# Item tables moved behind the ranks with four segments, and products in pairs on two halves of TensorE's rows

## The chip, the cores and the metric

The kernel runs on one core of one Trainium2 chip. The metric is the device time of one execution in microseconds; the lower the better. TensorE is PE in the profile, with PEld for its weight loads, VectorE is DVE, ScalarE is ACT, GpSimd is POOL and SyncE is SP.

## The reference

A small graph network with 6250 nodes of 256 features and 100000 edges, sorted by destination. Cut to what matters here:

```python
x = x + L0_gnn(layernorm(x), src, dst, edge_weight)      # weighted sum of neighbours, two products, L2 norm
x = x + L0_ffn(layernorm(x))                             # shared MLP and 4 gated experts
# L1 gnn, on the normalised x; edge_index[0] is src, all nodes have batch 0
sums = segment_sum(edge_attr, src, num_segments=n)       # 64 attributes per edge, summed by source
counts = segment_sum(ones, src, num_segments=n)
edge_attr_agg = sums / maximum(counts, 1.0)[:, None]
combined = concatenate([x, edge_attr_agg, u[batch]], axis=1)
x = x + (relu(combined @ W1 + b1) @ W2 + b2)             # 448 -> 512 -> 256
x = x + L1_ffn(layernorm(x))                             # 8 experts, the best 2 of each row
```

## The kernel before

**Rows and edges.** Nodes stand in 49 tiles of 128 (`NT`), in seven groups of seven (`NG`, `G`). Edges stand in 784 columns of 128 (`NC`), a run is four columns (`RUN`). An item is one run against one tile: the run's edges are made one-hot over the tile's 128 nodes by VectorE, PE multiplies the one-hot with the edges' rows, and VectorE adds the product to the tile's sum. A run with edges of several tiles is several items.

**The first block: aggregation by destination.** GpSimd gathers the source rows of a run from DRAM (L341, an indirect DMA per column) into one of seven slots (`SLOTS`), ScalarE weighs them (L401), VectorE makes the one-hots (`onehots`, L546) and sums (L558), PE multiplies (`products`, L649). GpSimd gathers into a slot again when PE has done with the run before in it (`s_mm` against row 3 of `row_i`). A loop step is eight items (`RING`). Steps run to item 96 (`FIRST`), then to 200 (`UNTIL`), then to 248 (`NI_A`).

Beside this work the edges are ranked by source. ScalarE counts the edges below each tile's first node (`source_count`, L391), in each segment of the columns (`SEGMENTS`) apart. After item 96 VectorE turns the counts into starts and offsets, and for each of three segments it makes the item tables: `runs_of_tiles`, `item_tables` (about 20 small instructions), PE turns two columns of `tab` into a row (`in_rows`, L628), VectorE copies it to `row4_i`. PE's steps from item 96 on wait for `s_row` 2, which follows the third table. Then, from item 96 to 200, VectorE makes four ranks in each step (`ranks`: a mask L595, one scan in each segment L598, a copy L603), 52 in all. SyncE loads the first attributes after `s_rank` 1 and stores the tables after `s_row` 2. GpSimd starts the first 16 scatters behind its gathers.

**The second block: dense layers beside the scatter.** GpSimd scatters the edges' attributes, one column of 128 edges per indirect DMA (L894, 768 times), into `sorted_edges` in DRAM, by rank; meanwhile the other engines do the layers L0. Then comes the aggregation by source: ScalarE's queue loads sorted edges (L1015, 16 slots `STEP4`), VectorE makes one-hots (L1347) and sums (L1356), PE multiplies (L1179). Each segment is sorted by itself, so its loads may start once its columns have landed (`LANDED`), and it has as many items as runs plus `NT` - 1 = 48: 160, 104 and 76, in sum `NL` = 340. ScalarE waits for a segment's columns before the steps of 16 items from `ITS4_FROM[n]` on:

```python
ITS4_FROM = tuple(sum(ITEMS4[:n]) // STEP4 for n in range(len(SEGMENTS)))
```

**The third block: the second GNN and the experts.** For each group g of seven tiles: ScalarE spreads the reciprocals of the counts (L1607), PE's `reciprocals` (L1705) brings them into the shape of the sums, VectorE's `node_columns` (L1840) multiplies them into the means, 64 partitions (`EA`) by 512 and 384 nodes. PE's `hidden` (L1715) multiplies the means, four times 128 outputs by two halves of the nodes, into four banks of PSUM, VectorE adds the parts made earlier (`add_parts`, L1846), ScalarE applies the ReLU (L1613), and PE's `node` (L1729) makes a tile's output, 28 products in a group. VectorE adds it to x (L1857), takes statistics (L1849, L1865) and makes the experts' gates; ScalarE writes the rows normalised by these (`gate_rows`, L1620), in its queue ahead of the next group's ReLUs. SyncE loads an expert's second weights in each group (`second_weights`, L1453), the parts (L1457), and stores x. Then follow the experts' blocks up to the end.

Of the kernel before, what the change touches and what calls it, by code (L numbers as in the profile page):

```python
# [6 lines left out]
P = 128  # L7
# [4 lines left out]
G = 7  # L12
# [29 lines left out]
SEGMENTS = ((0, 448), (448, 672), (672, NC))  # L42
# [77 lines left out]
def build(nc, a, out):  # L120
# [9 lines left out]
    with ctx:  # L130
# [77 lines left out]
        if True:  # L208
# [26 lines left out]
            starts = sb("starts", [P, NB + 1], f32, ph)  # L235
# [42 lines left out]
            with nc.Block() as block:  # L278
                @block.sync
                def _(sp):  # L280
# [17 lines left out]
                    sp.wait_ge(s_row, 2)  # L298
# [119 lines left out]
                def _(dve):  # L418
# [53 lines left out]
                    def runs_of_tiles(edges_per_run):  # L472
                        shift = edges_per_run.bit_length() - 1
                        own.add(nc.vector.tensor_copy(st_i[:, :], starts[:, :]))
                        own.add(nc.vector.tensor_scalar(up_i[:, :], starts[:, :], float(edges_per_run - 1), None, ALU.add))
                        own.add(nc.vector.tensor_tensor(nz[:, :], starts[:, 1:NB + 1], starts[:, 0:NB], ALU.is_gt))
# [99 lines left out]
                    for n, (c0, c1) in enumerate(SEGMENTS):  # L576
                        own.add(nc.vector.tensor_copy(starts[:, :], psum[:, 0, n * P:n * P + NB + 1]))
                        own.sync()
                        own.add(nc.vector.tensor_tensor(base[:, n, 0:NB], psum[:, 1, n * P:n * P + NB], starts[:, 0:NB], ALU.add))
                        own.sync()  # L580
                        own.add(nc.vector.tensor_scalar(base[:, n, 0:NB], base[:, n, 0:NB], float(c0 * P - 1), None, ALU.add))
                        runs_of_tiles(P * RUN)
                        item_tables(c0 // RUN, c1 // RUN)
                        dve.sem_inc(s_tab, 1)
                        dve.wait_ge(s_tabT, 2 + n)
                        i0, i1 = sum(ITEMS4[:n]), sum(ITEMS4[:n + 1])
                        own.add(nc.vector.tensor_copy(row4_i[:, :, i0:i1], psum[0:1, 2 + n, :].rearrange("p (k i) -> p k i", k=2)[:, :, 0:i1 - i0]))
                        own.sync()
# [23 lines left out]
                    with dve.Fori(UNTIL // RING, NI_A // RING) as it:  # L612
# [3 lines left out]
                def _(pe):  # L616
# [41 lines left out]
                    last.then_inc(s_off, 1)  # L658
                    for n in range(len(SEGMENTS)):
                        pe.wait_ge(s_tab, 2 + n)  # L660
                        in_rows(2 + n, (0, 1)).then_inc(s_tabT, 1)
                    pe.wait_ge(s_row, 2)
# [1456 lines left out]
```

## Time and profile before

| | us |
|---|---|
| median of 3 runs | 3086.56 |
| lowest, highest | 3085.42, 3093.0 |
| the profiled execution | 3096.71 |
| its span | 3095.0 |
| PE busy | 2492.1 |
| POOL busy | 1833.0 |
| DVE busy | 1404.5 |
| ACT busy | 927.9 |

The span goes from the first to the last instruction of the profiled execution; its time holds a little more. A busy share is a mean over stages with different limits: what an instruction is worth is read in its own stage, from the wait that ends last there. A line of the timeline gives the start, the duration, the engine, the line in the kernel, the operation and how many it merges, and in brackets how long the engine stood idle before it and what ended that.

### The profile page before, as it was taken

The page shows a single profiled execution, that of the slowest core. Times are in us where ns is not written, and L with a number is a line of the kernel's source. Part 1 is how long each engine was busy: PE and PEld are TensorE (multiplying, and loading weights), DVE is VectorE, ACT ScalarE, POOL GpSimd, SP SyncE. Part 2 cuts the span into 40 slices and gives each one's busy share as a digit, 9 for nine tenths or more (in the row PEclk, how much of TensorE's full clock was granted, in tenths as well). Part 3 has the DMA queues.
Part 4 walks back from the last instruction along what each step waited for, and adds up shares of the span by engine and source line. Part 5 has one row for each costly group of instructions (what it writes and reads, how often), then busy time and mean ns, then how long its engine had stood idle before and what let it go on. Part 6 is the DMA issues. An engine that isn't in the chain of part 4 may idle for free. (4 is left out here: it accounts for less than half of the span.)

```text
span 3095.0 us, 48451 instructions
## 1 busy us (share of the span) xinstructions
PE 2492.1 (81%) x11766; PEld 1963.1 (63%) x11767; DVE 1404.5 (45%) x3627; ACT 927.9 (30%) x2240; POOL 1833.0 (59%) x1907
## 2 busy tenths in 40 slices
PE   2556665666667589999999795839989999999998
PEld 1344444544555456666665794837668888888898
DVE  5222224988863233433433794836783222222222
ACT  4665333333333234444343000001542111111122
POOL 6777777777777777777777777770355222222222
PEclk9778776788888789999999897968999999999999
DMA  6333334333333312222222674632675444444464
GB/s 244 105 104 104 104 104 125 105 104 104 104 105 104 99 55 75 69 75 79 75 79 75 187 196 124 200 94 83 225 251 148 120 105 117 122 106 117 117 175 136
DMA packets 216588, 372.91 MB, mean 120 GB/s; under 512 B 50437, under 2 KB 133694, under 8 KB 215231
## 3 DMA queue, kind: packets, MB, share of 16 engines
q0 software_dynamic: 82928, 157.51, 19.2%
q1 hardware_dynamic: 75772, 154.16, 15.2%
q10 hardware_dynamic: 57812, 60.35, 6.7%
q8 instruction: 33, 0.54, 0.1%
q14 instruction: 43, 0.35, 0.0%
HBM read 290.16 MB, written 81.71 MB: 120 GB/s over the span
## 5 line engine op out<-in xcount | busy, mean ns | idle before, releaser
L649 PE MATMUL psum<-arena 128*128 x1984 | 621.6, 478 | 361.1 <-ACT arena L401 341.6
L341 POOL DMA_INDIRECT arena<-xn_rows,arena x784 | 747.4, 953 | 249.4 <-issue 234.8
L894 POOL DMA_INDIRECT sorted_edges<-arena x768 | 742.2, 966 | 249.0 <-issue 226.6
L649 PEld LDWEIGHTS psum<-arena 128*128 128x128 f32 x1984 | 463.7, 241 | 518.9 <-issue 436.1
L401 ACT ACTIVATE arena<-arena 128x256 f32<-128x256 f32 x784 | 334.0, 496 | 578.0 <-DMA arena<-xn_rows,arena 578.0
L1179 PE MATMUL psum<-arena,acc 128*65 128x128 f32 x2720 | 312.7, 277 | 107.9 <-DVE arena L1347 107.7
L1179 PEld LDWEIGHTS psum<-arena,acc 128*65 128x65 f32 x2720 | 301.6, 140 | 118.8 <-DVE arena L1347 112.0
L1347 DVE SCALAR_TENSOR_TENSOR arena<-psum,acc 128x512 f32<-128x512 f32 x340 | 252.8, 744 | 110.8 <-DMA acc<-sorted_edges 93.2
L1778 PE MATMUL psum<-arena,xr 128*128 x1344 | 299.1, 381 | 2.0 <-DVE xr L2008 2.0
L1765 PE MATMUL psum<-xr 128*128 128x256 f32 x1344 | 299.6, 381 | 0.9 <-DVE xr L2002 0.9
L558 DVE TENSOR_TENSOR acc<-acc,psum 128x256 f32 x248 | 103.1, 416 | 431.6 <-PE psum L649 431.6
L1765 PEld LDWEIGHTS psum<-xr 128*128 128x128 f32 x1344 | 257.1, 191 | 36.7 <-DVE xr L2002 1.3
L1778 PEld LDWEIGHTS psum<-arena,xr 128*128 128x128 f32 x1344 | 253.1, 191 | 35.5 <-issue 2.4
L1547 POOL DMA_INDIRECT out_y_dram<-xr,acc x84 | 130.9, 1558 | 217.7 <-ACT xr L1656 204.2
L546 DVE SCALAR_TENSOR_TENSOR arena<-psum,arena 128x512 f32<-128x512 f32 x252 | 187.7, 746 | 46.1 <-issue 37.5
L2008 DVE TENSOR_SCALAR xr<-psum,arena 128x256 f32<-128x256 f32 x168 | 73.6, 479 | 231.2 <-PE psum L1765 229.8
L1094 PE MATMUL psum<-arena 128*128 128x512 f32 (+1 forms) x336 | 158.3, 636 | 0.0
L1532 POOL DMA_INDIRECT dispatched<-acc,arena x98 | 94.4, 963 | 107.8 <-DVE arena L1902 62.2
L1656 ACT ACTIVATE xr<-xr,acc 128x256 f32<-128x256 f32 x84 | 42.6, 508 | 348.6 <-DVE xr L2014 348.6
L1607 ACT ACTIVATE arena<-ident,rcount 128x128 f32<-128x128 f32 x49 | 15.0, 387 | 437.1 <-PEq L818 427.0
L1542 POOL COPY acc<-acc 128x18 f32<-128x18 f32 x43 | 8.6, 200 | 217.6 <-DVE xr L2002 211.4
L2014 DVE TENSOR_TENSOR xr<-psum,acc 128x256 f32<-128x256 f32 x84 | 35.6, 424 | 218.9 <-PE psum L1778 218.9
(318 smaller groups left out, 3147.7 us busy)
## 6 DMA issues: line engine op xcount, KB each, us to landing
xr<-in_f_W_dram SPq DMA_DIRECT2D x63, 1024.0 KB, 5.1
acc<-sorted_edges ACTq DMA_DIRECT2D x340, 132.0 KB
arena<-in_attr_dram SPq DMA_DIRECT2D x98, 264.0 KB, 2.8
arena<-xn_rows,arena POOLq DMA_INDIRECT x784, 2.7
sorted_edges<-arena POOLq DMA_INDIRECT x784
arena<-hidden_parts SPq DMA_DIRECT2D x7, 1792.0 KB, 8.5
arena<-dispatched SPq DMA_DIRECT2D x42, 265.0 KB, 2.7
arena<-in_f_W_dram SPq DMA_DIRECT2D x8, 1024.0 KB, 11.5
```

The lines of the kernel that those rows point to most:

```text
L341: pool.indirect_dma_start(out=rows[:, c, :], out_offset=None, in_=xn_d, in_offset=bass.IndirectOffsetOnAxis(ap=idx[:, c:c + 1], axis=0)).t ...
L401: last = nc.scalar.activation(row, row, ACT.Copy, scale=w_c[:, ds((it * SLOTS + u) * RUN + c, 1)])
L546: nc.vector.scalar_tensor_tensor(hot[:, u, :, :], iota_p.unsqueeze(1).to_broadcast([P, RUN, P]), tile_b0[:, ds(i, 1)], dst_c[:, ds((run - ...
L558: nc.vector.tensor_tensor(there, there, psum[:, bank(u), 0:D], ALU.add).then_inc(s_acc, 1)
L649: last = nc.tensor.matmul(psum[:, bank(u), 0:D], hot[:, u, c, :], rows[:, ds(slots[k] + c, 1), :].squeeze(1), start=c == 0, stop=c == RUN - 1)
L894: pool.indirect_dma_start(out=edges_d, out_offset=bass.IndirectOffsetOnAxis(ap=pos_i[:, c:c + 1], axis=0), in_=stage[:, q % PARTS, c % SC, ...
L1094: last = nc.tensor.matmul(psum[:, b + m % 3, 0:w], w1[:, j, m, :], yT[:, j, columns(c)], start=j == 0, stop=j == 1)
L1179: last = nc.tensor.matmul(psum[0:EA + 1, bank4(u), 0:P], rows4[:, u, c, 0:EA + 1], hot4[:, u % RING, c, :], start=c == 0, stop=c == RUN - 1)
L1347: nc.vector.scalar_tensor_tensor(hot4[:, u % RING, :, :], iota4.unsqueeze(1).to_broadcast([P, RUN, P]), tile_b[:, ds(it * STEP4 + u, 1)], ...
L1547: pool.indirect_dma_start(out=out["y"], out_offset=bass.IndirectOffsetOnAxis(ap=wide_meta[:, u, h, 0:1].bitcast(i32), axis=0), in_=wide_y[ ...
L1765: last = nc.tensor.matmul(psum[:, 1 + m // 2, m % 2 * W:(m % 2 + 1) * W], wide_w[:, u, c, m * P:(m + 1) * P], wide_xT[:, c, :], start=c == ...
L1778: last = nc.tensor.matmul(psum[:, 5 + h, 0:D], wide_hT[:, m, h * P:(h + 1) * P], fw2[:, ds(e, 1), m, :].squeeze(1), start=m == 0, stop=m = ...
```

## The change

The columns are cut into four segments, 512, 128, 64 and 80 columns, with 176, 80, 64 and 68 items, in sum 388. The starts, offsets and bases of all segments are made after item 96 as before; the item tables are made after item 200, one after each of four steps of eight items, turned in a bank of PSUM that the ranks no longer need. `starts` is kept for each segment. SyncE waits for `s_row` 3 before it stores the tables; attributes are loaded as before after `s_rank` 1.

In the third block SyncE first copies the sums of groups 1 to 6 from partitions 0 to 63 to partitions 64 to 127 (`twice`), six DMAs. `reciprocals` brings the reciprocals to 128 partitions, `node_columns` scales both copies and waits in group 1 for the six DMAs. The weights `gw1e` are loaded twice, one copy for each half. In groups 1 to 6 every second product of `hidden` takes the upper half of rows. Products 5 and 7 no longer wait for a sum; products 4 and 6 wait for two.

```diff
-SEGMENTS = ((0, 448), (448, 672), (672, NC))
+SEGMENTS = ((0, 512), (512, 640), (640, 704), (704, NC))
...
-                    sp.wait_ge(s_row, 2)
+                    sp.wait_ge(s_row, 3)
                     sp.dma_start(item_d.unsqueeze(0), row4_i[:, :, :]).then_inc(s_rst, 16)
...
                     for n, (c0, c1) in enumerate(SEGMENTS):
-                        own.add(nc.vector.tensor_copy(starts[:, :], psum[:, 0, n * P:n * P + NB + 1]))
-                        own.sync()
-                        own.add(nc.vector.tensor_tensor(base[:, n, 0:NB], psum[:, 1, n * P:n * P + NB], starts[:, 0:NB], ALU.add))
-                        own.sync()
+                        own.add(nc.vector.tensor_copy(starts[:, n, :], psum[:, 0, n * P:n * P + NB + 1]))
+                    own.sync()
+                    for n, (c0, c1) in enumerate(SEGMENTS):
+                        own.add(nc.vector.tensor_tensor(base[:, n, 0:NB], psum[:, 1, n * P:n * P + NB], starts[:, n, 0:NB], ALU.add))
+                    own.sync()
+                    for n, (c0, c1) in enumerate(SEGMENTS):
                         own.add(nc.vector.tensor_scalar(base[:, n, 0:NB], base[:, n, 0:NB], float(c0 * P - 1), None, ALU.add))
-                        runs_of_tiles(P * RUN)
-                        item_tables(c0 // RUN, c1 // RUN)
-                        dve.sem_inc(s_tab, 1)
-                        dve.wait_ge(s_tabT, 2 + n)
-                        i0, i1 = sum(ITEMS4[:n]), sum(ITEMS4[:n + 1])
-                        own.add(nc.vector.tensor_copy(row4_i[:, :, i0:i1], psum[0:1, 2 + n, :].rearrange("p (k i) -> p k i", k=2)[:, :, 0:i1 - i0]))
-                        own.sync()
+                    own.sync()
                     dve.sem_inc(s_row, 1)
                     dve.sem_inc(s_rank, 1)
...
-                    with dve.Fori(UNTIL // RING, NI_A // RING) as it:
+                    for n, (c0, c1) in enumerate(SEGMENTS):
+                        for half in range(2):
+                            products(UNTIL + n * RING, half)
+                        runs_of_tiles(P * RUN, n)
+                        item_tables(c0 // RUN, c1 // RUN)
+                        dve.sem_inc(s_tab, 1)
+                        dve.wait_ge(s_tabT, 2 + n)
+                        i0, i1 = sum(ITEMS4[:n]), sum(ITEMS4[:n + 1])
+                        own.add(nc.vector.tensor_copy(row4_i[:, :, i0:i1], psum[0:1, RING - 2, :].rearrange("p (k i) -> p k i", k=2)[:, :, 0:i1 - i0]))
+                        own.sync()
+                    dve.sem_inc(s_row, 1)
+                    with dve.Fori(UNTIL // RING + len(SEGMENTS), NI_A // RING) as it:
...
+                    pe.wait_ge(s_row, 2)
+                    with pe.Fori(FIRST // RING, UNTIL // RING) as it:
+                        products(it)
                     for n in range(len(SEGMENTS)):
+                        products(UNTIL // RING + n)
                         pe.wait_ge(s_tab, 2 + n)
-                        in_rows(2 + n, (0, 1)).then_inc(s_tabT, 1)
-                    pe.wait_ge(s_row, 2)
-                    with pe.Fori(FIRST // RING, NI_A // RING) as it:
+                        in_rows(RING - 2, (0, 1)).then_inc(s_tabT, 1)
+                    with pe.Fori(UNTIL // RING + len(SEGMENTS), NI_A // RING) as it:
                         products(it)
...
+            twice = sums[0:2 * EA, :, :]
...
+                    for g in range(1, NG):
+                        sp.dma_start(twice[EA:2 * EA, g * G:(g + 1) * G, :], twice[0:EA, g * G:(g + 1) * G, :]).then_inc(s_deg_in, 16)
...
-                            nc.tensor.matmul(psum[0:EA, n, 0:c1 - c0], ones[:, 0:EA], spread[:, c0 // P:c1 // P, :].rearrange("p k n -> p (k n)"),
+                            nc.tensor.matmul(psum[0:2 * EA, n, 0:c1 - c0], ones[:, 0:2 * EA], spread[:, c0 // P:c1 // P, :].rearrange("p k n -> p (k n)"),
...
-                            if q >= 4:
-                                pe.wait_ge(s_hadd, g * 8 + q - 3)
-                            mean = aggT[0:EA, ds(g * G + c0 // P, (c1 - c0) // P), :].rearrange("p k n -> p (k n)")
-                            nc.tensor.matmul(psum[:, 4 + q % 4, 0:c1 - c0], gw1e[:, m, :], mean, start=True, stop=True).then_inc(s_h5, 1)
+                            if q >= 4 and q % 2 == 0:
+                                pe.wait_ge(s_hadd, g * 8 + q - 2)
+                            low = EA * (q % 2) if g else 0
+                            mean = twice[low:low + EA, ds(g * G + c0 // P, (c1 - c0) // P), :].rearrange("p k n -> p (k n)")
+                            nc.tensor.matmul(psum[:, 4 + q % 4, 0:c1 - c0], gw1e[low:low + EA, m, :], mean, start=True, stop=True).then_inc(s_h5, 1)
...
+                            if g == 1:
+                                dve.wait_ge(s_deg_in, 32 + 16 * (NG - 1))
+                            high = 2 * EA if g else EA
```

## Rows read from the trace of the kernel before

**Rows 1.** The waits of all engines: us in total, times, longest us.
```profile
DVE arena L1347 <- DMA acc<-sorted_edges: 93.2, 2, 55.2
...
POOL arena L341 <- PE psum L649: 14.6, 37, 3.6
```

**Rows 2.** The timeline around the item tables: start us, us, engine, line.
```profile
487.76 3.78 PE L649 MATMUL psum<-arena 128*128 x8 [3.04 <-ACT arena L401]
...
500.74 1.87 PE L628 MATMUL psum<-ident,arena 128*1 128x128 f32 x8 [4.59 <-DVEq L584]
...
518.18 12.15 PE L649 MATMUL psum<-arena 128*128 x41 [2.13 <-ACT arena L401]
...
522.74 0.95 POOL L341 DMA_INDIRECT arena<-xn_rows,arena  x1 [3.64 <-PE psum L649]
```

**Rows 3.** The timeline of the aggregation by source, VectorE.
```profile
1727.66 3.79 DVE L1347 SCALAR_TENSOR_TENSOR arena<-psum,acc 128x512 f32<-128x512 f32 x5
...
1913.92 0.75 DVE L1347 SCALAR_TENSOR_TENSOR arena<-psum,acc 128x512 f32<-128x512 f32 x1 [38.01 <-DMA acc<-sorted_edges]
...
2058.67 0.75 DVE L1347 SCALAR_TENSOR_TENSOR arena<-psum,acc 128x512 f32<-128x512 f32 x1 [55.20 <-DMA acc<-sorted_edges]
...
2138.08 0.28 DVE L1356 TENSOR_TENSOR acc<-acc,psum 65x128 f32 x1 [0.21 <-DVE acc L1356]
```

**Rows 4.** Groups by line, VectorE, from 2077.7 to 2122.1 and 2003.5 to 2139.
```profile
L1347 DVE SCALAR_TENSOR_TENSOR arena<-psum,acc 128x512 f32<-128x512 f32 x48 | 35.7, 743 | 2.4 <-PE psum L1179 1.9
...
L1347 DVE SCALAR_TENSOR_TENSOR arena<-psum,acc 128x512 f32<-128x512 f32 x84 | 62.5, 743 | 59.3 <-DMA acc<-sorted_edges 55.2 <-PE psum L1179 2.5 <-issue 0.6
```

**Rows 5.** The timeline of the third node group.
```profile
2204.92 6.25 PE L1715 MATMUL psum<-acc 64*128 64x512 f32 x16 [0.68 <-DVE xr L1857]
...
2206.73 5.03 DVE L1846 TENSOR_TENSOR arena<-psum,arena 128x512 f32<-128x512 f32 x8
...
2206.85 3.55 ACT L1620 ACTIVATE acc<-xr,arena 128x256 f32<-128x256 f32 x7 [0.47 <-DVE arena L1870]
...
2210.31 4.57 ACT L1613 ACTIVATE arena<-arena 128x512 f32<-128x512 f32 x8
...
2211.10 1.72 PE L1705 MATMUL psum<-arena,ones 128*64 128x512 f32 x4
...
2212.91 7.00 PEld L1729 LDWEIGHTS psum<-arena 128*128 128x128 f32 x32 [0.75 <-ACT arena L1613]
...
2226.81 6.25 PE L1715 MATMUL psum<-acc 64*128 64x512 f32 x16 [0.68 <-DVE xr L1857]
```

**Rows 6.** The rank stretch: busy us of PE, PEld, DVE, ACT, POOL; PEclk; DMA.
```profile
530.00:700.00 170.00, 113.04 (x377) 86.96 (x375) 145.96 (x214) 58.90 (x145) 128.60 (x135) 0.80 0.36 104
```

**Rows 7.** Groups by line, GpSimd, from 1063 to 1950 and 1915 to 2000.
```profile
L894 POOL DMA_INDIRECT sorted_edges<-arena x687 | 663.9, 966 | 223.3 <-issue 204.0 <-DMA sorted_edges<-arena 18.9 <-POOL arena L881 0.4
...
L894 POOL DMA_INDIRECT sorted_edges<-arena x66 | 63.8, 966 | 23.3 <-issue 21.7 <-DMA sorted_edges<-arena 1.6
```

**Rows 8.** Timeline of the first node group; DMA issues (KB, us to landing).
```profile
2143.30 0.40 SPq L1453 DMA_DIRECT2D arena<-in_f_W_dram  x1
...
2168.40 0.68 DVE L1840 TENSOR_TENSOR acc<-acc,psum 64x512 f32<-64x512 f32 x1 [1.34 <-PE psum L1705]
...
arena<-hidden_parts SPq DMA_DIRECT2D x7, 1792.0 KB, 8.5
```

**Rows 9.** Timeline of PE in groups five and six; two stretches of six.
```profile
2264.29 5.61 PE L1729 MATMUL psum<-arena 128*128 128x264 f32 x24
...
2288.05 7.28 PE L1729 MATMUL psum<-arena 128*128 128x264 f32 x24
...
2284.60:2288.00 3.40, 1.94 (x11) 1.34 (x9) 2.85 (x18) 1.49 (x2) 2.49 (x4) 1.00 1.01 354
...
2288.00:2291.40 3.40, 3.39 (x11) 2.73 (x11) 3.37 (x18) 0.00 (x0) 0.53 (x1) 0.65 0.74 269
```

**Rows 10.** The timeline of the first node group, PE.
```profile
2150.27 3.25 PE L1705 MATMUL psum<-arena,ones 128*64 128x512 f32 x4 [0.82 <-DVE arena L1833]
```

More of the change, by code:

```diff
@@ L234, in build @@
             cnt = sb("cnt", [P, len(SEGMENTS), NB], f32, ph)
-            starts = sb("starts", [P, NB + 1], f32, ph)
+            starts = sb("starts", [P, len(SEGMENTS), NB + 1], f32, ph)
             st_i = sb("st_i", [P, NB + 1], i32, ph)
@@ L471, in _, with runs_of_tiles @@
                     own.sync()
-                    def runs_of_tiles(edges_per_run):
+                    def runs_of_tiles(edges_per_run, n):
                         shift = edges_per_run.bit_length() - 1
-                        own.add(nc.vector.tensor_copy(st_i[:, :], starts[:, :]))
-                        own.add(nc.vector.tensor_scalar(up_i[:, :], starts[:, :], float(edges_per_run - 1), None, ALU.add))
-                        own.add(nc.vector.tensor_tensor(nz[:, :], starts[:, 1:NB + 1], starts[:, 0:NB], ALU.is_gt))
+                        own.add(nc.vector.tensor_copy(st_i[:, :], starts[:, n, :]))
+                        own.add(nc.vector.tensor_scalar(up_i[:, :], starts[:, n, :], float(edges_per_run - 1), None, ALU.add))
+                        own.add(nc.vector.tensor_tensor(nz[:, :], starts[:, n, 1:NB + 1], starts[:, n, 0:NB], ALU.is_gt))
                         own.sync()
@@ L744, in build @@
             run6 = sb("run6", [P, NX], f32, ph6)
[L745 removed]
+            gw1e = spare[0:2 * EA, 3 * G * ED + D:3 * G * ED + D + 4 * P].rearrange("p (m n) -> p m n", m=4)
             u0 = sb("u0", [P, 1], f32, ph6)
@@ L854, in _ @@
                         for dst, src in (
-                            (gw1e[:, :, :], a["g_W1"][D:D + EA, :].rearrange("p (m n) -> p m n", n=P)),
+                            (gw1e[0:EA, :, :], a["g_W1"][D:D + EA, :].rearrange("p (m n) -> p m n", n=P)),
+                            (gw1e[EA:2 * EA, :, :], a["g_W1"][D:D + EA, :].rearrange("p (m n) -> p m n", n=P)),
                             (gw1u, a["g_W1"][D + EA:D + EA + P, :].rearrange("p (m n) -> p m n", n=P)),
@@ L900, in _ @@
                         pool.wait_ge(s_hxo[c], NG * 16)
-                    pool.wait_ge(s_w3, 16 * (19 + 10))
+                    pool.wait_ge(s_w3, 16 * (19 + 11))
                     for g in range(NG):
@@ L1599, in _ @@
                 def _(act):
-                    act.wait_ge(s_w3, 16 * (19 + 10))
+                    act.wait_ge(s_w3, 16 * (19 + 11))
                     def deviation(ln, g, s_v, s_sd):
@@ L1691, in _ @@
                 def _(pe):
-                    pe.wait_ge(s_w3, 16 * (19 + 10))
+                    pe.wait_ge(s_w3, 16 * (19 + 11))
                     for m in range(4):
@@ L1838, in node_columns @@
                             dve.wait_ge(s_t5, PHASES * 2 + g * 2 + n + 1)
-                            mean = aggT[0:EA, ds(g * G + c0 // P, (c1 - c0) // P), :]
-                            nc.vector.tensor_tensor(mean, mean, psum[0:EA, n, 0:c1 - c0].rearrange("p (k n) -> p k n", n=P), ALU.mult).then_inc(s_tc5, 1)
+                            if g == 1:
+                                dve.wait_ge(s_deg_in, 32 + 16 * (NG - 1))
+                            high = 2 * EA if g else EA
+                            mean = twice[0:high, ds(g * G + c0 // P, (c1 - c0) // P), :]
+                            nc.vector.tensor_tensor(mean, mean, psum[0:high, n, 0:c1 - c0].rearrange("p (k n) -> p k n", n=P), ALU.mult).then_inc(s_tc5, 1)
                     def add_parts(g):
```

1 line of the change is left out of this document (removed).

## The prediction, on record before the result

> **What bounds the kernel now.** I read the page first, for the order of the stages: GpSimd is 70% or more busy in two long stretches, the gathers of node rows and the scatters of edge attributes, and PE is near full in the rest. Then came the waits, to see where each of the two parts of the change touches a queue that somebody waits for.
>
> First, the item tables. In the gather stage the GpSimd queue sets the pace: its longest wait for PE is 3.6 us, and the other waits charged to PE are the usual 0.30 us between two gathers [rows 1]. The reader is to see that the one long wait has a place: PE's products stop at 491.54 (487.76 + 3.78) and go on at 518.18, and GpSimd, which may run seven slots ahead, stops until 522.74 [rows 2]. In between VectorE makes three sets of tables and PE turns each into rows; one turn takes PE 1.87 us [rows 2].
>
> Second, the aggregation by source. VectorE idles 93.2 us in two waits for sorted edges, the second 55.2 us long [rows 1]; it starts again at 2058.67 and ends at 2138.36 [rows 3]. All that comes after the last scatter lies bare on the path, while the items before it are hidden behind the scatters. The group of lines after 2003.5 shows 84 one-hot instructions [rows 4]. The last segment has 28 + 48 = 76 items; the rest comes from `ITS4_FROM`, which divides 264 by 16 and rounds down to 16, so that the loads of items 256 to 263 stand behind the last wait too. 48 items from 2077.7 to 2122.1 took 44.4 us, so 0.926 us for one [rows 4].
>
> Third, the node groups of the second GNN. One group lasts 21.89 us (2204.92 to 2226.81) [rows 5]. PE's eight products L1715 take 6.25 us and its reciprocals L1705 end at 2212.82, but the next work, L1729 at 2212.91, is released by ScalarE's fourth ReLU: ScalarE writes seven rows (L1620, 3.55 us, from 2206.85) and only then the ReLUs (L1613, from 2210.31) [rows 5]. VectorE's eight sums L1846 run without a gap, 5.03 us from 2206.73 [rows 5]. So two engines other than PE set this stretch, and PE is level with ScalarE to within 0.09 us.
>
> **The change, part by part.**
>
> Tables moved. The stop of PE shrinks from 26.6 us to the offsets alone. From the last product before it to the first turn are 9.2 us (491.54 to 500.74), with the first table in them [rows 2]; two small products and a few copies come on top, which I put at 1 us, so the stop is at most some 10 us. One of 26.6 us cost GpSimd 3.34 us beyond its usual 0.30 [rows 2]: seven slots swallow some 23 us, and one of 10 us costs nothing: **-3.3 us**. Bounds: 0 (if another stall takes its place) and -3.6. The tables now stand behind the ranks, each after eight items. PE waited 4.59 us for one and took 1.87 us to turn it [rows 2], so a stop is 6.5 us, and far below the 23 us of the slots. The four are eight items apart, over which PE catches up. Without that cover they would cost 4 x 6.5 = 26 us. Behind the waiting VectorE stand the sums that free PE's banks, behind PE the slots. SyncE now holds the store of the tables until the fourth; only the attribute loads stand before it, and the store comes with 16 items still to go, before the stage's end.
>
> Four segments in ranks and counts. Each rank has one scan more, over the same columns in sum, so only its fixed part is added. No row shows that alone; below it is 0, above it is the mean of all of VectorE's instructions there, 146.0/214 = 0.68 us [rows 6]. An iteration of four ranks and eight items has 36 instructions, so 170 us hold 5.9 of them, each 28.6 us with 24.6 busy. Even at the upper end, 4 x 0.68 = 2.7 us fit into the 4.0 that are free: hidden behind the gathers, 0 us. Without that cover the upper end would cost 13 x 2.7 = 35 us, and GpSimd would feel only what the seven slots don't swallow. One Sign and accumulation more per count on ScalarE is hidden too, as that engine waits for gathered rows between its runs.
>
> Four segments in the aggregation. Items rise from 340 to 388, with 176, 80, 64 and 68; all the borders are multiples of 16, so the rounding is gone. Behind the last wait stand 68 instead of 84: 16 x 0.926 = **-14.8 us**. The 64 more before it (320 for 256) need cover. VectorE starts at 1727.66 [rows 3], now 3.3 us earlier, at 1724.4, and 320 x 0.926 = 296 us later, at 2020.7, it would be done, 35 us before the last edges (2058.67 - 3.3 = 2055.4). Are the middle segments there in time? By 1950 GpSimd had begun 687 scatters after the first 16, one in 1.291 us [rows 7]. Columns 512, 640 and 704 are then issued at 1704, 1869 and 1951, less 3.3; the loads of items 176, 256 and 320 wait for the columns 640, 704 and 784, and the items come up at 1887, 1961 and 2021. Each has 13 us or more, but the last. If a middle segment were late the 35 us would take it.
>
> Loads and scatters share the DMA engines. With loads beside them, 66 scatters have 63.8 + 23.3 = 87.1 us, 1.32 us each, against 1.291 over the whole [rows 7]. The loads now run 64 x 0.926 = 59 us longer beside them, some 46 scatters: between 0 and 46 x 0.03 = 1.4 us. The stretch of 85 us itself gives 1.29, so I stay near the low end, **+0.5 us**.
>
> The copies. SyncE issues six copies of aggregated means, 64 partitions by 3584 bytes, 224 KB each, 1.3 MB in sum, ahead of the expert's weights, from 2143.30 [rows 8]. VectorE's second call of `node_columns` waits for all. Before, it came at 2168.40 [rows 8], 25.1 us later. 1792 KB of hidden parts take 8.5 us [rows 8]; with six issues of some 0.5 us and the weights behind them I put landing at 10 to 15 us, hidden, 0 us. Bounds: no gain, and a loss only above 25 us; without the cover the 10 to 15 us would be bare. `node_columns` on 128 partitions instead of 64 costs as many columns, so the same.
>
> The pairs. If two products on the two halves of rows run beside each other, PE saves up to half of 6.25 us in each of six groups, 19 us of work. But by rows 5 the next products wait for ScalarE at 2212.91, whatever PE does before; the saving gives 0 (0.09 x 6 = 0.5 at most). If they do not run side by side, nothing changes either: the coarser waits of products 4 and 6 ask for sums that end at 2208.0 and 2209.3, and the last product is still done before its sum at 2211.1. The Trainium skill, TensorEngine Tiling (Array Packing), Performance Considerations, says that such tiling speeds up TensorE but not the evacuation of PSUM, which can then be the bottleneck. By this rule the part is worth nothing as well; the trace agrees, with 5.03 us of sums without a gap.
>
> What the pairs can cost is the clock. A pair takes 6.25/8 = 0.8 us. PE would work two pairs, stand until 2208.0, work the other two with a gap between, then 1.7 us of reciprocals, then stand some 1.3 us for ScalarE: 4 x 0.8 + 1.7 = 4.9 of 8.0 us in which it is now all but full. In the sixth group PE stood still for 1.46 us, was busy 1.94 of 3.40 us, and the granted clock then read 0.65: 24 records of L1729 took 7.28 us instead of 5.61, **1.67 us** [rows 9]. A fall in each of the six groups would cost 10 us, none 0. The gaps are spread, not one, so I take the near end, one fall more: **+1.7 us**. The skill's page TensorE: Matmul & The Clock Gate, section HAM oscillation, names such a pattern of short bursts and waits as what makes the clock swing; by it the six falls would be the forecast, -7.6 instead of -15.9.
>
> Sum: -3.3 - 14.8 + 0.5 + 1.7 = **-15.9 us**. The profiled execution took 3096.71 us, of which 3095.0 are span: it would take 3080.8. It lies 10.2 above the median of the runs shown, 3086.56, so the median is expected at **3070.7 us**.
>
> **The rivals.**
>
> A: the clock falls in most groups. For it: [rows 9], and the drop in PE's busy share. Against: a fall is only seen where PE was idle 43% of a stretch, and half of what it slows is cover. Time: 3086.56 - 17.6 + 10.0 = 3079.0.
>
> B: the pairs do shorten the groups, since PE and ScalarE are level and VectorE's chain starts sooner. For it: PE ends only 0.09 us before ScalarE lets it go. Against: L1620 and four ReLUs do not depend on L1715. 6 x 3.1 = 18.7 us: 3070.7 - 18.7 - 1.7 = 3050.3.
>
> C, to the other side: the clock falls and stays low for whole groups. In the first group it is low from 2150 on although PE is all but full, and L1705 takes 3.25 us there against 1.72 [rows 5, 10]. A group's 56 records of L1729, at 5.61 us for 24, are 13.1 us [rows 9] and would take as much again; six of them 79: 3086.56 - 17.6 + 79 = 3148. It makes the kernel slower by over 0.3% from 17.6 + 9.3 = 27 us on, which is a little over two whole groups. Against it: the one fall of [rows 9] cost 1.67 us and not a group.
>
> D: the segment part does nothing, as a middle segment comes late or the last is loaded slowly. Then only the 3.3 us stay, less 1.7 and 0.5: 3085.5. Against: 35 us of cover.
>
> **How the numbers follow.** 0.3% (9.3 us) is about what a measurement of this kernel can tell from no change. Chances: forecast 0.66 (its own range 3066 to 3075), A 0.18, B 0.07, C 0.03, D 0.06. Forecast and B lie beyond 0.3%, and of A the part with falls in three to five groups, 0.12: faster 0.85; the rest of A and D: same 0.12; C: slower 0.03. The range goes from 3063 (no fall, and a little of B) to 3079 (A with all six falls); it leaves out most of B, C, D, and the ends of A.
>
> **What would show it.** After the change: no wait of `L341` for PE above 0.5 us; 68 one-hots after the last wait for edges, which is 30 to 38 us long; the end of the aggregation 16 to 20 us earlier; L1715 starting its last product sooner but L1729 still released by the ReLUs, and a group of 21.9 us, up to 1.7 more where the clock falls. I am wrong if a wait for `s_deg_in` shows at `node_columns`, if a middle segment shows a wait over 1 us, or if groups change by more than 2 us.

## The result, and the profile after

The kernel after takes 3071.73 us (median of 12 runs, 3063.92 to 3077.27), the kernel before 3090.64 us on the same chips (12 runs, 3081.32 to 3096.02). The ratio is 0.9937, with a 95% interval of 0.9926 to 0.9947: 19.5 us less (16.4 to 22.9). Forecast were 3070.7 us and a gain of 15.9, a ratio of 0.9948. The time lies in the range, 1.0 us above the forecast, and the gain is 3.0 us (by the medians, 18.9) to 3.6 us (by the ratio) larger than the sum said. The ratios and their intervals are an estimate over all the runs and can differ from the quotient of two medians, by up to 0.0015 in what follows. The profiled execution took 3076.77 us, with a span of 3074.7; the span before was 3095.0, so the two profiles are 20.3 us apart.

The waits of all engines after, as in [rows 1] (us in total, times, longest us):

```profile
DVE arena L1359 <- DMA acc<-sorted_edges: 32.1, 1, 32.1
...
POOL arena L341 <- PE psum L656: 11.0, 36, 0.3
```

One wait for edges is left out of two, and GpSimd's long wait for PE is gone. The timeline at the offsets, which answers to [rows 2]:

```profile
487.81 1.99 PE L656 MATMUL psum<-arena 128*128 x8 [1.69 <-ACT arena L401]
...
495.60 3.18 SPq L297 DMA_DIRECT2D arena<-in_attr_dram  x7
...
497.22 7.16 PE L656 MATMUL psum<-arena 128*128 x24 [3.63 <-issue]
...
504.62 3.39 ACT L401 ACTIVATE arena<-arena 128x256 f32<-128x256 f32 x8 [6.72 <-DMA arena<-xn_rows,arena]
505.94 0.95 POOL L341 DMA_INDIRECT arena<-xn_rows,arena  x1 [1.77 <-issue]
```

PE's products stop for 7.4 us (487.81 + 1.99 to 497.22) where they stopped for 26.6. But GpSimd has a new gap of 1.77 us at 505.94. Just before it ScalarE waits 6.72 us for gathered rows, and before that SyncE issues the seven loads of edge attributes. The tables behind the ranks, PE:

```profile
920.00 1.36 PE L635 MATMUL psum<-ident,arena 128*1 128x128 f32 x8 [4.30 <-DVEq L613]
...
948.51 1.86 PE L635 MATMUL psum<-ident,arena 128*1 128x128 f32 x8 [4.32 <-DVEq L613]
```

The four turns wait 4.19 to 4.32 us each, 27 to 29 us apart. The aggregation by source, which answers to [rows 3], and the group of its one-hot instructions from 2024 to 2120, which answers to [rows 4]:

```profile
1727.79 2.73 DVE L1359 SCALAR_TENSOR_TENSOR arena<-psum,acc 128x512 f32<-128x512 f32 x4
...
2054.57 0.75 DVE L1359 SCALAR_TENSOR_TENSOR arena<-psum,acc 128x512 f32<-128x512 f32 x1 [32.08 <-DMA acc<-sorted_edges]
...
2119.10 0.28 DVE L1368 TENSOR_TENSOR acc<-acc,psum 65x128 f32 x1 [0.21 <-DVE acc L1368]
```

```profile
L1359 DVE SCALAR_TENSOR_TENSOR arena<-psum,acc 128x512 f32<-128x512 f32 x68 | 50.6, 744 | 35.3 <-DMA acc<-sorted_edges 32.1 <-issue 2.0 <-PE psum L1191 0.9
```

From the last wait to the end are 64.8 us (2054.57 to 2119.38) instead of 79.7. The timeline of the third node group after, which answers to [rows 5]:

```profile
2186.99 1.99 PE L1730 MATMUL psum<-acc 64*128 64x512 f32 x8 [0.68 <-DVE xr L1875]
...
2188.79 4.51 DVE L1864 TENSOR_TENSOR arena<-psum,arena 128x512 f32<-128x512 f32 x8
...
2190.13 0.92 PE L1730 MATMUL psum<-acc 64*128 64x384 f32 x4 [1.16 <-DVE arena L1864]
...
2192.18 1.77 PE L1719 MATMUL psum<-arena,ones 128*128 128x512 f32 x4
2192.37 4.57 ACT L1627 ACTIVATE arena<-arena 128x512 f32<-128x512 f32 x8
...
2194.97 7.41 PE L1744 MATMUL psum<-arena 128*128 128x264 f32 x32 [1.02 <-ACT arena L1627]
...
2208.87 1.13 PE L1730 MATMUL psum<-acc 64*128 64x512 f32 x4 [0.68 <-DVE xr L1875]
```

The pairs do run side by side: the first four products take 1.99 us, where four of the same 512 columns took some 3.6 (their share by columns of the 6.25 for eight). PE then stands twice for VectorE, 1.16 and 0.28 us, and 1.02 us for ScalarE's ReLU. The group lasts 21.88 us (2186.99 to 2208.87), as before. The copies, which answer to [rows 8]:

```profile
2124.39 4.89 SPq L1465 DMA_DIRECT2D acc<-acc  x6
...
2149.71 0.69 DVE L1858 TENSOR_TENSOR acc<-acc,psum 128x512 f32<-128x512 f32 x1 [1.45 <-PE psum L1719]
```

Nobody waits for them: the reader 25.3 us later is released by PE.

The 20.3 us between the profiles come together so. The last gather comes 1.5 us earlier (1033.0 for 1034.5). The scatters take 2.6 us less, so at the last wait it is 4.1. The last segment brings 14.9, so at the end of the aggregation it is 19.0. The first node group is 0.9 us longer (29.75 for 28.87), four groups are equal, the sixth is 2.3 shorter (23.16 for 25.44), and 0.1 to 0.2 go either way behind and before them.

### The profile page after: what moved, and what is told of

The parts are those of the page before. It is cut to its first block and busy times, and to the rows that moved or that the text cites. A ratio compares the mean times of both kernels' runs of the same rounds, so it can differ in the third digit from the quotient of the medians.

```text
span 3074.7 us, 50036 instructions
## 1 busy us (share of the span) xinstructions
PE 2517.9 (82%) x12162; PEld 1993.4 (65%) x12163; DVE 1454.9 (47%) x3798; ACT 941.9 (31%) x2340; POOL 1833.4 (60%) x1907
## 3 DMA queue, kind: packets, MB, share of 16 engines
q1 hardware_dynamic: 76332, 155.66, 15.4%
## 5 line engine op out<-in xcount | busy, mean ns | idle before, releaser
L1191 PE MATMUL psum<-arena,acc 128*65 128x128 f32 x3104 | 354.7, 276 | 46.6 <-DVE arena L1359 46.4
L1191 PEld LDWEIGHTS psum<-arena,acc 128*65 128x65 f32 x3104 | 340.6, 139 | 60.6 <-DVE arena L1359 50.8
L1359 DVE SCALAR_TENSOR_TENSOR arena<-psum,acc 128x512 f32<-128x512 f32 x388 | 288.4, 744 | 50.0 <-DMA acc<-sorted_edges 32.1
```

The source lines that it names most:

```text
L1191: last = nc.tensor.matmul(psum[0:EA + 1, bank4(u), 0:P], rows4[:, u, c, 0:EA + 1], hot4[:, u % RING, c, :], start=c == 0, stop=c == RUN - 1)
L1359: nc.vector.scalar_tensor_tensor(hot4[:, u % RING, :, :], iota4.unsqueeze(1).to_broadcast([P, RUN, P]), tile_b[:, ds(it * STEP4 + u, 1)], ...
```

## The experiments

**One part at a time.** Four kernels, each against the kernel before, whose median there was 3091.49. Without the pairs:

```diff
-                            low = EA * (q % 2) if g else 0
-                            mean = twice[low:low + EA, ...]
+                            mean = aggT[0:EA, ...]
...
-                    for g in range(1, NG):
-                        sp.dma_start(twice[EA:2 * EA, ...], twice[0:EA, ...])
```

> The change without its second part: four segments and moved tables, but one copy of the means and one product after another. Theory (the pairs lie behind ScalarE's ReLUs and give nothing by themselves): 0.994 to 0.996 of the kernel before, within 3 us of the full change, the end of the aggregation at 2119 as in the full change, and node groups of 21.9 us; the sixth group may fall into the low clock again and be 25.4 us instead of 23.2. Rival (the pairs give what the result has beyond the forecast): 3 us or more slower than the full change, and longer in every group, not only the sixth.

Measured: 3076.48 us, ratio 0.9954 (0.9939 to 0.9968); one wait of 33.2 us. Its fourth group lasted 26.77 us and not 21.9. The timeline of PE there, and two stretches of it (busy us of PE, PEld, VectorE, ScalarE and GpSimd, granted clock, DMA share, GB/s):

```profile
2202.39 9.76 PE L1725 MATMUL psum<-acc 64*128 64x512 f32 x16 [0.68 <-DVE xr L1867]
2212.08 3.24 PE L1715 MATMUL psum<-arena,ones 128*64 128x512 f32 x4
```

```profile
2203.00:2206.40 3.40, 3.40 (x8) 1.50 (x7) 2.68 (x12) 2.38 (x6) 2.79 (x3) 0.79 0.99 329
2206.40:2209.80 3.40, 3.40 (x6) 1.67 (x5) 1.42 (x3) 3.40 (x8) 2.48 (x4) 0.50 0.48 166
```

The same eight products that take 6.25 us in [rows 5] take 9.76 here, because the granted clock falls to 0.50, the 1.2 GHz level, while PE is busy without a gap. That costs 4.9 us of this profile. By the ratios this kernel is 5 us slower than the whole, outside the 3 us of the theory, but only one group is longer and not every one, as the rival has it.

The segments without tables moved and without pairs, as three segments with the last border at 704:

```diff
-SEGMENTS = ((0, 448), (448, 672), (672, NC))
+SEGMENTS = ((0, 512), (512, 704), (704, NC))
```

> The kernel before with only the borders of its three segments moved, from columns 448 and 672 to 512 and 704; tables where they were, no pairs. 340 items as before, 176, 96 and 68 of them. Theory (only the number of items behind the last wait counts, 84 before and 68 now, each 0.926 us): 14 to 15 us faster, 0.995 to 0.9955; the middle segment is done at some 2042, before the last edges. Rival (a fourth segment is needed to keep the middle items in time): the last wait for edges disappears and the end comes at 2130 or later, less than 9 us faster.

Measured: 3080.53 us, ratio 0.9966 (0.9953 to 0.9979). Its two waits for edges sum to 77.0 us, the longest 63.2, and the last one-hot starts at 2120.4 instead of 2135.4, 15.0 us earlier, so a fourth segment is not needed for this. The ratio gives less than the trace, 10.5 us (6.5 to 14.5), and less than the theory's 0.995 to 0.9955. The profile has a long group, 4.8 us; whether the other runs have one too is not shown:

```profile
2233.50 9.64 PE L1715 MATMUL psum<-acc 64*128 64x512 f32 x16 [0.68 <-DVE xr L1857]
```

The tables behind the ranks, three segments in their old places, no pairs:

```diff
-SEGMENTS = ((0, 512), (512, 640), (640, 704), (704, NC))
+SEGMENTS = ((0, 448), (448, 672), (672, NC))
```

> Only the item tables moved behind the ranks, with the three segments of before, 84 items behind the last wait, no pairs. Theory: the long stop of the gathers goes but for a short one that the attribute loads bring along, 1 to 3 us faster, within 0.1%; the aggregation ends some 1 to 4 us earlier. Rival (moving the tables frees more, up to the scatters): 4 us or more faster.

Measured: 3089.29 us, ratio 0.9992 (0.9981 to 1.0003). The last gather comes at 1032.3, 2.2 us earlier than before, and the last one-hot starts 1.0 us earlier (2134.4). By its time alone the gain can't be told from none.

The pairs alone, on the kernel before (its diff is that of the first experiment, turned round):

> The kernel before with only the second part: copies of the means and products in pairs. Theory: nothing in groups two to five (21.9 us each), and at most 2 to 3 us in the sixth group, where PE waits for VectorE and the clock fell before: between 3 us faster and 1 us slower. Rival A (short bursts of PE let the clock fall): 5 to 10 us slower. Rival B (the groups shorten): 6 us or more faster.

Measured: 3087.5 us, ratio 0.9991 (0.9982 to 0.9999), so 2.8 us less (0.3 to 5.6). The second to the fifth group last 21.88 to 21.89 us, and the sixth 23.37 instead of 25.44, as the theory has it.

The middle values of the parts, 0.9966, 0.9992 and 0.9991, multiply to 0.9949, and the whole is 0.9937 (0.9926 to 0.9947). The intervals of the parts are wide enough for the 0.0012 between them. The segment edit carries most of it.

**All rows of TensorE, one product after another.** (From here to the later border, before: 3095.09.) In all node groups but the first each product of the aggregated means now contracts all 128 partitions, both copies at half value; the sum is the same.

```diff
-                            low = EA * (q % 2) if g else 0
-                            mean = twice[low:low + EA, ...]
+                            high = 2 * EA if g else EA
+                            mean = twice[0:high, ...]
```

> The full change, but in groups 1 to 6 each product of hidden takes all 128 rows (both copies of the means at half their value, both copies of the weights), one after another: PE's work is 6.25 us again, on full rows instead of half. Theory (products on 64 rows let the granted clock fall or keep it low even when PE is busy without a gap, and that is what the pairs save): no group of 26.7 us, all of 21.9 but the sixth, and a time within 2 us of the full change. Rival (the pairs help by freeing PE, or the falls come from elsewhere): the time is that of the change without pairs, 4 to 5 us slower, and groups of 26.7 us are seen.

Measured: 3072.31 us, ratio 0.9941 (0.9923 to 0.9959). A group of it:

```profile
2198.99 6.25 PE L1731 MATMUL psum<-acc 128*128 128x512 f32 x16 [0.68 <-DVE xr L1876]
2205.08 1.67 PE L1720 MATMUL psum<-arena,ones 128*128 128x512 f32 x4
2206.98 7.41 PE L1745 MATMUL psum<-arena 128*128 128x264 f32 x32 [0.23 <-ACT arena L1628]
```

Products on 128 rows take the same 6.25 us as on 64, and with 6.25 us of PE in place of the 3.8 of the pairs (1.99 + 0.92 + 0.92) the group lasts the same 21.88 us. So what PE saves by running side by side does not shorten these groups. Whether full rows keep the clock up this kernel can't tell: single products on 64 rows have no long group in four profiles of six either.

**ReLUs ahead of the row part.** If ScalarE's order is the bound, the pairs pay only once that is changed:

```diff
                     for g in range(1, NG):
                         deviation(ln6, g - 1, s_v6, s_sd6)
+                        hidden(g)
                         gate_rows(g - 1)
-                        hidden(g)
```

> The full change with ScalarE's ReLUs of a group ahead of its writing of the normalised rows of the group before. Theory (ScalarE's rows hide what the pairs save on PE): L1744 starts 7.0 instead of 8.0 us after the first product, groups of some 20.9 us, 4 to 6 us faster than the full change. Rival (another engine bounds the group): groups of 21.9 us, no gain.

> The change without pairs, with the ReLUs first. Theory: PE's eight products and the reciprocals end 7.9 us after the first product, so groups stay at 21.8 us and at most 1 us is gained over the change without pairs; the pairs are worth 5 us or more beside this. Rival: as fast as with pairs.

Measured: with pairs 3068.61 us, ratio 0.9917 (0.9899 to 0.9936); without 3071.45 us, 0.9936 (0.9919 to 0.9952). A group with pairs:

```profile
2184.66 1.99 PE L1730 MATMUL psum<-acc 64*128 64x512 f32 x8 [0.76 <-DVE xr L1875]
...
2187.19 4.58 ACT L1627 ACTIVATE arena<-arena 128x512 f32<-128x512 f32 x8 [1.07 <-DVE arena L1864]
...
2189.85 1.77 PE L1719 MATMUL psum<-arena,ones 128*128 128x512 f32 x4
...
2191.46 7.31 PE L1744 MATMUL psum<-arena 128*128 128x264 f32 x32
...
2205.36 1.99 PE L1730 MATMUL psum<-acc 64*128 64x512 f32 x8 [0.78 <-DVE xr L1875]
```

The wait of L1744 for ScalarE is gone, and a group lasts 20.70 us (2184.66 to 2205.36); without pairs the same order gives 21.73. So ScalarE's order hid 1.2 us of what the pairs save in a group. By the ratios the pairs are worth 6 us here, but the two intervals overlap. Not all of the gain is kept: the four earlier groups save 4.6 us against the kernel after, and the sixth lasts 24.88 us instead of 23.16. In it PE waits longer for VectorE, and the products behind the wait take 7.28 us instead of 5.60:

```profile
2263.21 0.39 PE L1734 MATMUL psum<-arena,ones 128*128 128x8 f32 x2 [2.18 <-DVE arena L1904]
...
2263.84 7.28 PE L1744 MATMUL psum<-arena 128*128 128x264 f32 x24
```

**A later border.** Borders at 512, 640 and 736, with a wait at half a step so that the rounding does no harm (its lines are left out here):

```diff
-SEGMENTS = ((0, 512), (512, 640), (640, 704), (704, NC))
+SEGMENTS = ((0, 512), (512, 640), (640, 736), (736, NC))
```

> The full change with borders 512, 640 and 736, and the loads' wait for a segment's columns at a half step of eight items, so that exactly 60 items stand behind the last columns. Theory: the third segment starts at some 1991, when column 736 has landed, and its 72 items end at some 2058, just after the last columns; the wait there is 0 to 4 us; 60 x 0.926 = 56 us later the aggregation ends, at some 2114, 4 to 6 us before that of the full change. Rival (middle items come late): it ends at 2118 or later, no gain.

Measured: 3074.03 us, ratio 0.9936 (0.9919 to 0.9953). VectorE's only wait has moved to the segment before the last:

```profile
1997.42 0.75 DVE L1365 SCALAR_TENSOR_TENSOR arena<-psum,acc 128x512 f32<-128x512 f32 x1 [35.00 <-DMA acc<-sorted_edges]
```

```profile
L1365 DVE SCALAR_TENSOR_TENSOR arena<-psum,acc 128x512 f32<-128x512 f32 x132 | 98.2, 744 | 40.8 <-DMA acc<-sorted_edges 35.0 <-PE psum L1197 3.7 <-issue 0.7
```

From 1997.42 on, 132 items run without another wait for edges, and the last one-hot starts at 2117.9, where it is 2116.5 in the kernel after: the third segment has become the late one, and the rival holds. Of the two last borders tried, 704 and 736, neither is shown to be faster; borders between them were not tried.

**The last four** (before: 3092.25). The attribute loads of SyncE moved behind the ranks:

```diff
-                    sp.wait_ge(s_rank, 1)
+                    sp.wait_ge(s_rank, 3 * NRANK + 1)
                     for h in range(PARTS):
                         sp.dma_start(stage[:, h, :, :], ...)
```

> The whole change, and SyncE's first seven loads of edge attributes (L297) wait until all ranks are made (s_rank at 3 x NRANK + 1, at 899.9 in the kernel after) instead of for the first 1 (495.60). In the kernel after one gap of GpSimd is left behind the offsets, 1.77 us at 505.94, and ScalarE's runs wait 6.72 us for gathered rows at 504.62, after the attribute loads of 495.60. Theory A, the loads delay the gathered rows: the gap at 506 goes, the last gather comes at 1031.5 (after: 1033.0) and nothing shows near 900, where GpSimd's slots are full again; the whole is 1.5 us shorter, too little to tell by its time. Rival B, the gap is left by PE's stop of 7.4 us at 489.8: it stays at 506, at 1.8 us. Rival C, the gap goes with the loads, wherever they are: 1.5 to 2 us near 900.

Measured: 3068.62 us, ratio 0.9925 (0.9912 to 0.9939), the last gather at 1033.4. The timeline near 900:

```profile
898.70 3.22 SPq L297 DMA_DIRECT2D arena<-in_attr_dram  x7
...
907.57 1.70 ACT L401 ACTIVATE arena<-arena 128x256 f32<-128x256 f32 x4 [7.14 <-DMA arena<-xn_rows,arena]
908.88 0.95 POOL L341 DMA_INDIRECT arena<-xn_rows,arena  x1 [1.92 <-issue]
```

At 506 GpSimd now issues every 1.26 us without a gap, and the gap stands at 908.88, as long as it was. The kernel after has no gap near 909. Rival C is right: the seven loads can take this time from the gathers in both places.

The whole change with three segments:

```diff
-SEGMENTS = ((0, 512), (512, 640), (640, 704), (704, NC))
+SEGMENTS = ((0, 512), (512, 704), (704, NC))
```

> The whole change with three segments of columns, borders 512 and 704, instead of four with 512, 640 and 704: the last segment is the same, 68 items behind the last wait. Theory, the fourth segment gives only cover: VectorE waits twice, 70 to 80 us in sum, the last wait 55 to 65 us instead of 32.1, one-hot products end at 2118 to 2121, and the time is that of the kernel after, ratio to before 0.993 to 0.995. Rival, the segment between is needed, so that the loads of the second segment with 704 columns come too late: one-hots end over 3 us later, ratio 0.9955 or more.

Measured: 3068.73 us, ratio 0.9923 (0.9909 to 0.9937); the waits are 76.8 us in two, the longest 63.6, and the last one-hot starts at 2115.0. No gain of the fourth segment is seen: what counts here is where the last border lies.

The kernel without pairs once more:

> The same kernel as tables_4seg_no_pairs once more: tables behind the ranks and four segments, products of the aggregated means one after another on 64 rows. It asks how often the clock falls within these products. Theory, products on 64 rows are where the clock falls with PE fully busy: a group of 26 to 27 us is seen again in one of groups 1 to 4 (two of the four such profiles so far that don't have the ReLUs first), and the time is 3 to 5 us above the kernel after, ratio to before 0.995 to 0.996. Rival, the two long groups were luck that pairs have as often: all groups 21.9, ratio 0.9935 to 0.9945.

Measured: 3070.29 us, ratio 0.9933 (0.9919 to 0.9946), the second to the fifth group at 21.88 to 21.89 us (the expectations count the groups from 0). The rival holds for this profile.

The ReLUs first, three segments and the late attribute loads together:

> The version that the runs so far point to: pairs, the next group's products of the aggregated means before its row part on every engine's queue as in relu_first_pairs (groups 20.7), three segments with borders 512 and 704, and the attribute loads behind the ranks. If the parts add: ratio to before 0.9915 less 0.0005 for the attribute loads, so 0.991, 3066 to 3069 against a before of 3093; groups of 20.7 us, one-hots end at 2117 to 2119. Rival, the parts don't add (the attribute loads disturb the gathers elsewhere or the second segment is late): 0.993 or more.

Measured: 3071.16 us, ratio 0.9932 (0.9918 to 0.9945). The second to the fifth group last 20.66 to 20.80 us, as meant, but the sixth lasts 26.50 us, and the whole gains nothing. The ratio is the rival's, its causes are not: the last one-hot starts at 2117.6, as the theory has it, and the loss is in the node groups. In that group:

```profile
2261.93 0.55 PE L1734 MATMUL psum<-arena,ones 128*128 128x8 f32 x2 [2.28 <-DVE arena L1904]
...
2262.76 8.59 PE L1744 MATMUL psum<-arena 128*128 128x264 f32 x24
```

```profile
2259.30:2262.70 3.40, 1.12 (x6) 0.77 (x5) 2.88 (x17) 1.49 (x2) 2.64 (x3) 0.90 1.05 363
2262.80:2270.00 7.20, 7.20 (x20) 5.69 (x21) 5.13 (x28) 0.00 (x0) 3.14 (x4) 0.58 0.36 132
```

PE waits 2.28 us for the counts that VectorE makes at the end of its chain for the experts. It is busy 1.12 us of 3.40, the clock falls behind that, and 24 records of L1744 take 8.59 us instead of 5.61. The kernel after has the same wait with 0.74 us and no fall (clock 1.00, records 5.60 us). Of 4.7 us that the earlier groups save, 3.3 go here. The other kernel with pairs and the ReLUs first has the same loss, with 2.18 us of wait and 7.28 us of records. PE is ready for the counts 1.3 us sooner there (14.1 us after the group's start instead of 15.4), but the counts come no sooner, 16.3 to 16.4 us after it. No kernel here is shown to beat the one after. The fastest by its middle value, with the ReLUs first, has an interval up to 0.9936, and this kernel, which contains its edit, did not repeat it.

## Why the prediction was right, point by point

**Tables, -3.3 forecast.** The step that the stop shrinks below what seven slots swallow holds: the stop is 7.4 us, against "at most some 10", the wait for PE of 3.6 us is gone, and the turns behind the ranks (4.2 to 4.3 us of wait, 1.87 of work) show in no wait of GpSimd. The size was off. The last gather gains 1.5 us, not 3.3, since the attribute loads now have a gap of their own, 1.77 us. 1.5 + 1.77 is the 3.3 of the forecast, though a match to the tenth is luck. Of the nine profiles with the tables moved and the loads near 500, three have no such gap, and their last gather comes at 1031.5 to 1031.8, 2.7 to 3.0 us earlier than before; six have one of 0.9 to 2.0 us, and theirs comes at 1032.3 to 1034.2. Without the tables moved it comes at 1034.2 to 1034.8 (three profiles). So the stop itself is worth nearly the 3.3 us, and a collision that comes in most profiles but not in all takes part of it. Before, these loads came at 516.57, where GpSimd was kept back by PE, so the stall had covered them. The forecast said that they stood ahead of the store in SyncE's queue, and did not ask what they collide with once they start 21 us earlier. It had given 0 as a bound for just that, another stall in its place. That these loads cause the gap is shown by the two profiles with late loads: both have it near 909, 1.92 and 1.98 us, where none of the others has one. What spares the three near 500, and how loads that take 3.2 us to issue delay the gathered rows, is not shown.

**Last segment, -14.8 forecast.** 14.9 in the kernel after, 15.0 in the borders alone. 68 one-hots stand behind a wait of 32.1 us, forecast as 30 to 38. The cover, the time that VectorE has done all earlier items before the last edges come, was 32 us against the 35 of the sum. This term is most of the change: the borders alone gave 0.9966, 10.5 us (6.5 to 14.5).

**Scans and the fourth segment, 0.** Right: nothing shows. But no gain of the fourth segment is seen either, 0.9923 (0.9909 to 0.9937) with three.

**Scatters, +0.5.** From the first to the last scatter are 987.1 us after, 989.8 before. The other profiles have 984.9 to 991.5 in both kinds: three segments 985.4 to 991.5, four segments 984.9 to 989.0. So the 2.6 us lie within the spread of one profile to the next, and the contention of 0 to 1.4 us is too small to be seen in it. Rows of two profiles can't be compared to less than some 3 us there.

**Copies, 0.** Right; cover 25.3 us, no wait.

**Pairs, 0 in the group.** Right, by the mechanism given: L1744 is still released by the ReLU, the group is 21.88 us, and with the ReLUs ahead of the rows it falls to 20.70 while that without pairs stays at 21.73. Against rival B stands also the kernel with full rows, whose groups are equal with 6.25 us of products instead of 3.83. The Trainium skill, TensorEngine Tiling (Array Packing), Performance Considerations, says that tiling may only shift the limit to what empties PSUM. The trace agrees in part: PE waits 1.16 and 0.28 us for VectorE's sums, 4.51 us in all, but what lets the next work go is ScalarE's ReLU, and that follows from the order of ScalarE's queue.

**Clock, +1.7 forecast: the step that failed, with its sign.** The reading was that pauses between pairs bring the clock down. In seven profiles with pairs the second to the fifth group, 28 in all, have no fall, although PE stands there for 1.16 and 0.28 us in each, and in five of the seven profiles for 1.0 us more. The falls are on the other side: two of 24 such groups with single products on 64 rows, both with PE busy without a gap, 4.8 and 4.9 us each. Two of 24 against none of 28 may be chance.

In the sixth group, where [rows 9] showed a fall of 1.67 us, the kernel after has one fall less and not one more. It lasts 23.16 us instead of 25.44, and a group that changes by more than 2 us was one of the prediction's own signs of being wrong. PE waits there for the counts that VectorE makes. With pairs VectorE's sums take 4.51 us instead of 5.03, the counts come 16.1 us after the group's start instead of 16.9, and PE's wait is 0.74 us instead of 1.46. In the eight profiles with a wait of 0.74 to 1.24 us there, the 24 records of `node` behind it take 5.60 us; in the six with 1.34 to 2.28 us they take 7.28 to 8.59. That points to the wait as the cause of the fall, but no kernel changed the wait by itself. The pairs alone take the fall away (23.37 us, 2.8 us less in time, 0.3 to 5.6). But so do the borders alone, with single products (23.67 us, a wait of 1.24). With the borders moved and ScalarE's order kept, the pairs leave 23.16 to 23.35 us there and single products 23.64 to 23.67, and the two measurements of the kernel without pairs gave 0.9954 and 0.9933 against 0.9937 of the whole. So no cost of the pairs is seen, and the forecast fall did not come; how much of 0 to 5 us they give is open.

The Trainium skill, TensorE: Matmul & The Clock Gate, section HAM oscillation, has bursts with longer waits between them as what makes the clock swing. The pauses of the pairs, 1.16 us behind 1.99 us of products, are shorter than the bursts, so the six falls that the prediction read from that section go beyond it, and none was seen. The stretch with PE busy 1.12 of 3.40 us before the long sixth group is nearer to its case, and there the trace agrees: the clock fell.

Of the rivals, A (falls in most groups), B (groups shorten) and C (whole groups at the low level, slower) are excluded by the four groups of 21.88 us, and D (the segments do nothing) by the end of the aggregation. A part of B came true: VectorE's sums end 0.5 us sooner, which only the sixth group shows.

The sum by the trace: -1.5 and -14.9 for -3.3 and -14.8, -2.6 of spread for +0.5, and -1.3 of the node groups and what follows for +1.7. Against the forecast these are +1.8 (tables), -0.1, -3.1 (scatters) and -3.0 (clock), -4.4 in all; by the runs the gain was missed by 3.0 to 3.6 us. The time was missed by only 1.0 us, since the kernel before came out at 3090.64 us and not at the 3086.56 of three runs: that closeness is luck. Of the 4.4 us, 3.1 lie within the spread of the scatters, and the 0.9 us by which the first node group is longer depend on when the clock came back there.

## What to carry to other kernels

What runs behind the last arrival of a long transfer is bare: count its items, round included, and move the last border until the segment before it is only just in time; more segments than that brought nothing here. When a stall is removed, look at what else was issued in its shadow, loads of another queue above all, since they come earlier and may collide, as the attribute loads did here. And an engine made faster beside an equal one gives nothing until the order on the equal one is changed, and then the next chain can take much of it back: here the wait for VectorE's counts took 1.7 of 4.6 us in one kernel and 3.3 of 4.7 in the other.

## What the runs showed of the hardware

- Two products of 64 rows on the two halves of TensorE's rows run side by side: 1.99 us for four of 512 columns (0.5 us each), where one after another they are 3.57 us by columns (2048 of 3584 columns, of the 6.25 us of [rows 5]). A product on 128 rows takes no longer than one on 64, 6.25 us for the eight.
- The clock can fall, or stay down, while PE is fully busy with products on 64 rows; why is not shown. In all 14 profiles it falls to 0.50 in or just behind a pause of PE of 4.3 to 4.5 us before the node groups. In nine, the kernel after among them, the eight products of the first group run at 0.50 throughout, 12.31 us, and in the kernel after the clock is back only when products on 128 rows run, after 2152. In four (full rows, late attributes, and two without pairs) it is back just before the same products, and the group lasts 21.2 to 21.3 us instead of 28.3 to 29.9. In the last (ReLUs first, late attributes and three segments) it comes back, falls again within them, and they take 9.75 us. So one such moment moves a profile by some 8 us, more than all of the change but its largest term:

```profile
2135.36 12.31 PE L1730 MATMUL psum<-acc 64*128 64x512 f32 x16 [0.64 <-DVE acc L1858]
```

- Seven direct loads of the attributes can delay rows that another queue gathers. In eight of the eleven profiles with the tables moved, ScalarE waits 6.0 to 7.1 us for such rows instead of some 3.3, and GpSimd stands for 0.9 to 2.0 us instead of 0.30; in three it does not.
